# Second self-attention: the norm moves from GpSimd to ScalarE with offsets from VectorE for two tiles at a time, and the opening of the kernel is reordered

## What is computed

```python
x = x + tanh(g_xattn[0]) * cross_attention(layernorm(x), ctx)            # 16 heads of 8
inner = x
for l in range(2):
    inner = inner + self_attention_l(layernorm(inner, ln1_w[l], ln1_b[l]))   # causal, 16 heads of 8
    h = layernorm(inner, ln2_w[l], ln2_b[l])
    inner = inner + (token_moe, sequence_moe)[l](h)                          # 8 experts, the best two
x = x + tanh(g_ffn[0]) * inner
x = x + tanh(g_xattn[1]) * gated_recurrence(layernorm(x), ctx)
x = x + tanh(g_ffn[1]) * int8_product(layernorm(x))
```

## Time and profile before

| | |
|---|---|
| median of 3 runs | 1054.81 us (1050.97 to 1061.59) |
| the profiled execution, its run and its span | 1058.88 us, 1056.9 us |
| mean granted clock of TensorE | 0.924 |
| PE, PEld busy | 875.1, 711.3 us |
| DVE, ACT, POOL busy | 709.9, 689.9, 514.5 us |
| cross attention and first self-attention | about 16 to 313 us |
| routing, then the token experts | 313 to 514 us |
| fetches and second self-attention | 516.3 to 705.6 us |
| sequence experts, recurrence, int8 product | 706 to 1057 us |

### The profile page before, as it was taken

One profiled execution on the slowest core, in us unless ns is written; L12 is line 12 of the kernel. 1 busy time (PEld: TensorE's weight loads), 2 busy tenths in 40 slices (PEclk: granted clock), 3 DMA queues, 4 the chain that ended last, 5 costly groups with the idle time before them and its releaser, 6 DMA issues.

```text
span 1056.9 us, 34800 instructions
## 1 busy us (share of the span) xinstructions
PE 875.1 (83%) x11693; PEld 711.3 (67%) x11693; DVE 709.9 (67%) x1912; ACT 689.9 (65%) x1914; POOL 514.5 (49%) x893
## 2 busy tenths in 40 slices
PE   3999999999986599999458888975999998879804
PEld 2778878788875299999446776863777777747501
DVE  3488888888868856666458888768312122957795
ACT  2588888899973577777347887853555554448635
POOL 6133334566672155555389898411333332038616
PEclk9999999999997699999759999987999999979955
DMA  5000032000002022222211001800000001511002
GB/s 146 11 17 15 15 101 74 3 2 0 0 2 81 5 66 65 65 67 63 47 33 33 25 25 25 239 2 0 1 0 0 0 0 37 123 48 38 17 0 80
DMA packets 53195, 41.54 MB, mean 39 GB/s; under 512 B 11176, under 2 KB 45716, under 8 KB 53124
## 3 DMA queue, kind: packets, MB, share of 16 engines
q1 hardware_dynamic: 48220, 31.50, 10.8%
q0 software_dynamic: 4320, 8.86, 3.5%
q10 hardware_dynamic: 584, 0.26, 0.1%
HBM read 27.42 MB, written 9.24 MB: 35 GB/s over the span
## 4 chain that ended last, share of the span: by engine, by line
PE 56%; DVE 18%; POOLq 8%; issue 7%; POOL 6%; ACT 2%; SPq 2%; DMA 1%; DVEq 0%; ACTq 0%
PE ps_st L1207 14%; PE ps_o L1207 14%; PE ps_v L1309 8%; PE ps_xa L1207 8%; POOLq L830 5%; PE ps_v L1207 5%; PE ps_o L1331 3%; DVE work L1711 3%; POOL work L831 2%; POOLq L820 2%; DVE y L1725 1%; DVE recip L1722 1%; DVE stats L1650 1%; SPq L543 1%; POOL h_all L799 1%
## 5 line engine op out<-in xcount | busy, mean ns | idle before, releaser
L747 POOL TENSOR_TENSOR shared<-kts,kmask 128x256 f32<-128x256 f32 x192 | 135.9, 729 | 162.4 <-ACT qts L934 99.6
L1207 PE MATMUL ps_st<-work 128*128 128x128 f32 (+1 forms) x872 | 153.0, 319 | 16.7 <-POOL work L831 9.6
L1207 PEld LDWEIGHTS ps_st<-work 128*128 128x128 f32 x872 | 123.6, 191 | 40.5 <-POOL work L831 26.1
L965 ACT COPY probs_t<-ps_v 128x512 f32<-128x512 f32 x192 | 112.6, 586 | 47.8 <-PE ps_v L1309 45.8
L1703 DVE TENSOR_REDUCE rowmax<-ps_st 128x16 f32<-128x1024 f32 x96 | 117.2, 1221 | 28.3 <-PE ps_st L1207 26.0
L1309 PE MATMUL ps_v<-ident,work 128*128 128x128 f32 x768 | 123.5, 284 | 3.0 <-ACT probs_t L965 2.2
L1711 DVE TENSOR_TENSOR work<-ps_st,rowmax 128x1024 f32<-128x1024 f32 x96 | 116.5, 1214 | 0.1
L789 POOL DMA_INDIRECT xg<-x_rows,row_from x71 | 76.7, 1081 | 78.9 <-PE ps_xa L1393 59.0
L957 ACT ACTIVATE work<-work 128x512 f32<-128x512 f32 x192 | 110.4, 622 | 2.3
L1207 PE MATMUL ps_o<-shared,probs_t 128*64 128x18 f32 x3072 | 109.3, 212 | 0.5
L1102 ACT ACTIVATE probs_t<-ps_st,b1s 128x256 f32<-128x256 f32 x152 | 59.7, 476 | 73.2 <-PE ps_st L1207 73.2
(11 more groups left out here) (379 smaller groups left out, 2086.9 us busy)
## 6 DMA issues: line engine op xcount, KB each, us to landing
y_rows<-work SPq DMA_DIRECT2D x71, 64.0 KB, 1.6
w<-in_L_ffn_e_w_dram SPq DMA_DIRECT2D x2, 2048.0 KB, 11.4
w<-rhs_const SPq DMA_DIRECT2D x2, 1536.0 KB, 11.2
x_res<-in_x_dram SPq DMA_DIRECT2D x4, 512.0 KB, 6.6
ctx_in<-in_ctx_dram SPq DMA_DIRECT2D x32, 64.0 KB, 1.8
x_rows<-h_all SPq DMA_DIRECT2D x1, 2048.0 KB, 9.9
ctx_dup<-in_ctx_dram SPq DMA_DIRECT2D x32, 64.0 KB, 1.8
out_dram<-x_res SPq DMA_DIRECT2D x16, 128.0 KB, 1.8
```

The source lines that it names most:

```text
L747: i = pool.tensor_tensor(km[:, par, g, :, :], kts[:, par, g:g + 1, :].to_broadcast([P, KM_HEADS, SEQ]), kmask[:, :, :], ALU.mult)
L965: nc.scalar.copy(probs_t[:, par, 512 * half:512 * half + 512], ps_v[:, :]).then_inc(S["pts_ready"], 1)
L1207: return nc.tensor.matmul(o, a, b, start=start, stop=stop, skip_group_check=True)
```

## The change

Two parts. **The norm of the second self-attention**: GROUP becomes 2, so LEAD is 5 and AHEAD 7. POOL's `normalise` goes. DVE makes the offset -mean x root for two tiles (`group_bias`), ACT norms with scale and offset (`normalise`, first in its iteration with lag 2), the attention on ACT is 2 later, and `group_root` goes from first to last. DVE's order is new: bias (first group only), combine_first, y, max, bias (other groups), combine_second, stats, sums, add, shift. **The opening**: the cross attention starts on the statistics of the first 8 tiles (FIRST), the other 24 are hooks in DVE's iterations 1 to 4, the means and roots of these at 5 to 7; context tiles come before the bulk of x and the small loads are dealt out between them; the setup pieces move to tiles 8 to 11 and `small_weights` to iteration 9; 8 more iterations are unrolled. One POOL semaphore (`slots_cast`) is merged into another.

```diff
-GROUP = 4
+GROUP = 2
@@ chained @@
-        stop = seg * n + head + (SEAM if seg else 0)
+        stop = seg * n + head + (SEAM if seg else opening)
@@ sync @@
-            for q in range(4):
-                a, b = q * (NT // 4), (q + 1) * (NT // 4)
-                sp.dma_start(x3[:, a:b, :], x_v[:, a:b, :]).then_inc(x_loaded[q], 16)
...
-            pipeline(sp, [(0, ctx_load(0))])
+            first_ctx = ctx_load(0)
+            x_load(0)
+            first_ctx(0, 0)
+            first_ctx(1, 1)
+            for q in range(1, 4):
+                x_load(q)
+            for t in range(2, 2 * SUB):
+                first_ctx(t, t % 2)
+                late_loads(t - 2)
...
+            with sp.Fori(SUB, NT // 2, 1) as turn:
+                for u in range(2):
+                    first_ctx(turn * 2 + u, u)
             expert_load(0)
@@ gpsimd @@
-            def normalise(t, par):
-
-                pool.wait_ge(S["rstd_ready"], CH_SELF1 + t // GROUP + 1)
-                seen(pool, S["xt_ready"], TB[1] + t - 1)
-                pool.tensor_scalar(xn[:, par, :], tile(inner, t), aggr[:, t, 0:1], rstd[:, t:t + 1],
-                                   ALU.subtract, ALU.mult).then_inc(S["xn_ready"], 1)
...
-            straight([(LEAD, normalise), (AHEAD, kbd_after_scores), (AHEAD - 1, four_biases), (0, fetch)])
+            straight([(AHEAD, kbd_after_scores), (AHEAD - 1, four_biases), (0, fetch)])
@@ scalar @@
-            row_root(CH_CROSS)
+            row_root(CH_CROSS, 0, FIRST)
...
+                    {6: lambda: row_root(CH_CROSS2, FIRST, NT),
...
+            def normalise(t, par):
+
+                act.wait_ge(S["fetched_bias"], t // GROUP + 1)
+                seen(act, S["xt_ready"], TB[1] + t - 1)
+                nc.scalar.activation(xn[:, par, :], tile(inner, t), ACT.Identity, bias=nbias[:, t:t + 1],
+                                     scale=rstd[:, t:t + 1]).then_inc(S["xn_ready"], 1)
+
-            straight([(0, group_root)] + attention(1, 1))
+            straight([(2, normalise)] + later(attention(1, 1), 2) + [(0, group_root)])
@@ tensor: setup_piece, and take_over on ACT likewise @@
-                if t == 2:
+                if t == 8:
...
-                elif t in (3, 4):
+                elif t in (9, 10):
...
-                elif t == 5:
+                elif t == 11:
@@ vector @@
+            x_sums(0, FIRST)
+            row_means(CH_CROSS, FIRST, 0, FIRST)
...
-            row_stats(CH_CROSS, NT)
+            row_rstd(CH_CROSS, 0, FIRST)
...
-                    {3: small_weights,
+                    {1: lambda: x_sums(FIRST, FIRST + 6), 2: lambda: x_sums(FIRST + 6, FIRST + 12),
+                     3: lambda: x_sums(FIRST + 12, FIRST + 18), 4: lambda: x_sums(FIRST + 18, NT),
+                     5: lambda: row_means(CH_CROSS2, NT, FIRST, NT), 7: lambda: row_rstd(CH_CROSS2, FIRST, NT),
+                     9: small_weights,
...
+            def group_bias(t):
+
+                dve.wait_ge(S["rstd_ready"], CH_SELF1 + t // GROUP + 1)
+                V.scalar_tensor_tensor(nbias[:, t:t + GROUP], aggr[:, t:t + GROUP, 0], -1.0, rstd[:, t:t + GROUP],
+                                       ALU.mult, ALU.mult).then_inc(S["fetched_bias"], 1)
+
+            def opening_bias(t, par):
+
+                if t == 0:
+                    group_bias(0)
+
+            def middle_bias(t, par):
+
+                if t and t % GROUP == 0:
+                    group_bias(t)
+
-            straight(later([sums_, y_, max_, add_, shift_], LEAD)
-                     + [(LAND, combine_first), (LAND, combine_second), (LAND, fetched_stats)])
+            straight([(LAND + GROUP, opening_bias), (LAND, combine_first)] + later([y_, max_], LEAD) + [(LAND + GROUP, middle_bias), (LAND, combine_second), (LAND, fetched_stats)]
+                     + later([sums_, add_, shift_], LEAD))
```

More of the change, by code:

```diff
@@ L151, in later, with chained @@
     return [(step[0] + lag,) + tuple(step[1:]) for step in steps if step]
-def chained(eng, segments, hooks=(), n=NT, unroll=4):
+def chained(eng, segments, hooks=(), n=NT, unroll=4, opening=8):
     hooks = dict(hooks)
@@ L450, in build @@
         NORM1 = MLSTM + ACT_GROUPS * SUB
-        EARLY = 20
-        CH_CROSS, CH_EARLY, CH_LATE, CH_PRE0, CH_SELF1 = range(5)
+        FIRST, EARLY = NT // 4, 20
+        CH_CROSS, CH_CROSS2, CH_EARLY, CH_LATE, CH_PRE0, CH_SELF1 = range(6)
         CH_PRE1, CH_M0, CH_M1, CH_N0, CH_N1 = (CH_SELF1 + NGROUP + k for k in range(5))
@@ L536, in _, with x_load, late_loads @@
             x3 = x_res[:, :].rearrange("p (t d) -> p t d", d=D)
-            for q in range(4):
+            def x_load(q):
                 a, b = q * (NT // 4), (q + 1) * (NT // 4)
                 sp.dma_start(x3[:, a:b, :], x_v[:, a:b, :]).then_inc(x_loaded[q], 16)
-            def late_loads():
-                for dst, src in small_loads:
+            def late_loads(k):
+                for dst, src in small_loads[k * LATE_EACH:(k + 1) * LATE_EACH]:
                     sp.dma_start(dst, src).then_inc(S["late_loaded"], 16)
-                sp.dma_start(b2b[:, :, :], A["L0_ffn_e_b2"][0:1, :, :].to_broadcast([P, NE, D])
-                             ).then_inc(S["b2b_loaded"], 16)
             def ctx_load(base):
                 def fn(t, par):
-                    if isinstance(t, int) and t == 2:
-                        late_loads()
                     seen(sp, S["ctx_used"], base + t - 1)
@@ L1939, in combine_second, with x_sums @@
                                        ALU.mult, ALU.add).then_inc(S["second_done"], 1)
-            for q in range(4):
-                dve.wait_ge(x_loaded[q], 16)
-                for t in range(q * (NT // 4), (q + 1) * (NT // 4)):
-                    sums_step(x_res)(t, 0)
+            def x_sums(a, b):
+                for q in range(4):
+                    part = range(max(a, q * (NT // 4)), min(b, (q + 1) * (NT // 4)))
+                    if part:
+                        dve.wait_ge(x_loaded[q], 16)
+                    for t in part:
+                        sums_step(x_res)(t, 0)
+            x_sums(0, FIRST)
+            row_means(CH_CROSS, FIRST, 0, FIRST)
             dve.wait_ge(S["setup_copied"], 3)
             V.tensor_scalar(coef[:, 0:1], tg[:, 0:1], ROW0_PAIRS, None, ALU.mult).then_inc(S["dve_setup"], 1)
-            row_stats(CH_CROSS, NT)
+            row_rstd(CH_CROSS, 0, FIRST)
             dve.wait_ge(S["dve_setup"], 1)
```

23 lines of the change are left out of this document (12 added, 11 removed).

## The result

| | before | after |
|---|---|---|
| median | 1056.95 us | 1098.87 us |
| runs | 1050.97 to 1061.59 (4) | 1089.92 to 1099.73 (4) |
| span of the profiled execution | 1056.9 us | 1098.0 us |
| ratio | | 1.037 (1.032 to 1.043) |

The changed kernel is 3.7% slower. The sign was forecast, the size was not: 1076.5 us, with a range to 1097.

A forecast was written before the change was run, and what follows sets the result against it. No engine is full; a loop of waits through DVE and PE sets 5.00 us a tile. Opening -5.0 and second self-attention +26.7 give +21.7, 1076.5 us against the median of 1054.81; range 1060 to 1097.

The forecast's parts named there:

- The loop: Second self-attention: ACT's copy of y waits for DVE's root inputs or bias alternately, 6.2 us a tile against 5.00; stage +26.7 us.
- The forecast's pair: Second self-attention: two alternating intervals, 5.61 with the bias next and 6.84 with the root next, 12.45 us for two tiles.
- The clock: PE's granted clock in the second self-attention, forecast at 1.00; its fall to the lower level was a rival, chance 0.17.
- The faster rival: Second self-attention: ACT's waits are hidden and DVE's chain paces at 4.62 us a tile, 1038 us; chance 0.13.
- The single wait: Second self-attention: only one ACT wait bites, 1050 us if the bias, 1064.6 us if the root; chance 0.10 together.
- Filling: Start of the second self-attention: first fetch to first add takes 36.5 us instead of 40.7, 4.2 earlier.
- The opening: Start of the kernel: first scores near 20.8 instead of 25.49, a gain of 5 us passed on, bounds 2.5 and 9.
- the upper bound of 9: Opening's largest gain in us, if setup pieces are cheaper at the high clock and the clock rises sooner.
- The range: Whole kernel: from 1060, terms at their cheap end, to 1097 for the clock, leaving out the faster rival and a tail.
- the clock rival: Second self-attention: PE falls to the lower clock in the new gaps, 20 us more, 1096 us; chance 0.17.

The follow-up runs named there:

- e13: Changed kernel, attention one iteration later so both ACT waits leave the loop, POOL's bias between its two fetches: ratio to before 0.986, 1041.2 us.
- e8: Changed kernel, attention one iteration later against combination and root, offset still made in the iteration that needs it, so only its wait remains: ratio to before 1.000.
- e9: e7 plus eight further transposes per tile that change nothing, filling PE's gap in the second self-attention: ratio to before 1.010.
- e4: Changed kernel plus eight further transposes per tile that change nothing, filling PE's gap in the second self-attention: ratio to before 1.016, 1090.1 us.
- e7: Changed kernel with ACT's norm moved behind the copy of y, so only the root's wait stays in the loop: ratio to before 1.025.
- e10: Changed kernel, attention one iteration later and bias made earlier, so both ACT waits are off the loop: ratio to before 0.994.
- e1: Changed kernel with the old second self-attention put back, leaving only the reordered opening: ratio to before 0.994.
- e12: Kernel before with only the reordered opening, repeated on another chip: ratio to before 0.993.
- e15: Kernel before with only the reordered opening, third time, on yet another chip: ratio to before 0.996.
- e11: e10 with POOL's bias of four tiles placed before its product for the scores: ratio to before 1.003.

## Why the prediction was right in kind and too low

**The loop: right.** Both waits are where the count of iterations put them, and each costs what removing it gives back. From quiet intervals:

| kernel | pair, us | above e13 |
|---|---|---|
| e13, no wait | 4.85 + 4.85 = 9.70 | |
| e8, offset's wait | 5.74 + 5.16 = 10.90 | 1.20 |
| e9, root's wait | 6.15 + 5.30 = 11.45 | 1.75 |
| changed kernel, both | 6.89 + 5.79 = 12.68 | 2.98 |

1.20 + 1.75 = 2.95: the two add up. The forecast's pair was 12.45, so 24 tiles at full clock take 12 x 12.68 = 152.2 us instead of the forecast 149.4. The 2.8 us are several small errors, here from start to start in two quiet intervals of the profile after. Longer were the norm, 0.51 and 0.50 instead of 0.39; the offset with its handing over, 0.37 instead of 0.22; and the stretch from the second combination to the logarithm, 1.04 instead of 0.94. Shorter were the way from the copy of y to the next maximum, 3.77 instead of 3.87, as the first probability copy starts 0.16 behind it and not 0.27, and the exponential, 0.11 instead of 0.20. The price of the offset itself was right, 0.15 us where nothing of POOL's runs beside it; it took 0.33, and the combination 0.47 instead of 0.34, because POOL's product for the scores ran beside them. The forecast costed POOL at nothing and had no such term.

**The clock: the step that failed.** The forecast put the stage's clock at 1.00 and gave PE's fall to the lower level, with +20 us and 1096 us, a chance of 0.17. It was this rival that happened. Of the 168.06 us, 168.06 - 152.2 = 15.9 are above the quiet pairs; filling the gap took back 11.1 of them in e4, and in e9 21.1 us against e7. That the other 4.8 are the clock's as well is likely, as e4's clock was still 0.95, but no run shows it. The forecast had seen the row that mattered: PE busy 72% of a window and the clock at 0.63 in the next, with 70% to be expected of the new loop. It set it aside because that window had no scores. After the change PE was busy 60% and 70% in the windows at 580 and 588, with scores, and 0.64 followed. The busy share alone doesn't tell, though: the kernel before held 1.00 from 608 to 616 us with PE busy 6.71 of 8 us, and e10 had 0.84 from 576 to 584 us with 6.77. The trace agrees with "TensorE: Matmul & The Clock Gate" of the Trainium skill (A second HAM failure mode) that short idle times between groups of matmuls are enough to make the clock swing.

Waits and clock together: 168.06 - 118.45 = 49.6 us, of which 152.2 - 118.45 = 33.7 are waits and 15.9 the clock. With both in the forecast, 1076.5 + 16 + 3 would have been 1095.

**The faster rival: fallen** for the changed kernel, as ACT has both waits. Its arithmetic was good, though: 4.62 us a tile without waits was 4.85 in e13, and there a stage of the new form is in fact shorter than the old.

**The single wait: fallen.** e7 and e8 have one each; the changed kernel has both. As a price for the offset's wait alone 10.23 a pair was given, measured 10.90; for the root's 11.46, measured 11.45 in e9. This close agreement is luck in part: in e9 the norm, priced at 0.39, no longer stands ahead of the copy of y, so the forecast's terms give 11.07 for it.

**Filling: half right.** 2.6 us instead of 4.2, as add(0) came 38.1 behind the first fetch instead of 36.5. The error is spread: the maxima of tiles 0, 1 and 2 started 20.6, 26.2 and 34.9 us behind the fetch instead of 20.4, 25.7 and 33.9, and the copy of y at 37.0 instead of 35.7.

**The opening: the sign and the reason right, the size small.** The scores came at 21.09, forecast 20.8. The forecast then let the 5 us pass on; they grew instead. PE's second half takes 0.63 us at 36.90 where it was 1.06 at 35.93 before: the first such pass of 0.60 us is at 28.32, before at 48.30, so the clock had risen some 20 us earlier, the second of the reasons given for the upper bound of 9. At the first fetch 8.2 us were left; of the whole kernel, 4 to 7 (e1, e12, e15). Where the rest goes is open.

**The range.** Its top was the clock rival's own 1096 plus one; the kernel took 1098.87 against a reference that was 2 us above the median the range was made for.

## What to carry to other kernels

When work moves to an in-order engine, count for each of its waits in which iteration of the other engine the awaited thing is made; one iteration more of lead was worth 3 us a pair here and, with POOL's bias moved too, turned a loss of 3.7% into a gain of 1.4%. Then ask of every new gap on PE whether the clock survives it: price the loop at both levels, and where a row shows a similar busy share followed by a fall, give the fall more than the chance of a tail. Last, look at what stands beside what on DVE and POOL: POOL's bias cost next to nothing beside DVE's shift, which reads PSUM, and 1 to 3 us beside a combination of two SBUF tiles.

## What the runs showed of the hardware

- **Useless work on PE can pay.** Eight more transposes a tile, and the clock rose from 0.76 to 0.97 (windows of e7 and e9, 560 to 660 us, two chips) and 24 tiles fell from 162.4 to 141.3 us.
- **DVE waits for POOL when its operands are SBUF tiles.** DVE's combination of two SBUF tiles took 0.34 us alone, 0.47 where it began as POOL's product was ending, 1.44 beside POOL's bias of 1.26 us, and 3.09 beside three of POOL in a row (2.63 us from 601.32 to 603.95). It was not let in between them (its record begins 0.3 us before POOL's, while DVE still runs the shift; POOL's spans are rough). Maximum and shift, which read PSUM, took 1.23 and 1.21 us beside POOL's work. "SBUF — State Buffer" of the Trainium skill (SBUF: two separate sides) says that a VectorE operation with two SBUF inputs and a GpSimd operation that reads SBUF share a pair of ports as an exclusive lock, held for the whole instruction; the traces agree, and add that instructions of POOL that follow one another closely keep the other side out over all of them.
- **The same lock more than doubles a small operation.** DVE's offset on 128x2 elements, both inputs in SBUF, took 0.15 us with nothing of POOL's beside it (at 522.14 in the profile after, at 605.65 in e11, where half of the offsets are such). Beside POOL's product it took 0.33: from 573.65 to 573.98 in the profile after, where the product ends at 573.97. Of the 14 offsets of that profile with the product beside them, 13 end within 0.02 us of its end. The product starts with the maximum, both released by PE's scores, so the offset right behind the maximum falls on the product's last 0.3 us in each pair.
- **Open:** on one chip the kernel with the reordered opening lost some 2.5 us at every fourth tile in PE's scores with nothing to wait for, and the kernel before took 1075.7 us there against 1058 elsewhere. The same kernel showed none of it on two other chips.
